# Flamingo block pair on one Trainium2 core: the openings of both attentions in another order

## What is computed

```python
x = x + tanh(g_xattn[0]) * L0_xattn(layernorm(x), ctx)       # 16 heads of 16, mask on the keys
x = x + tanh(g_ffn[0])   * L0_ffn(layernorm(x))              # 8 experts, top 2, and a shared one
x = x + tanh(g_xattn[1]) * L1_xattn(layernorm(x), ctx)       # attention, two norms, gelu layer
x = x + tanh(g_ffn[1])   * L1_ffn(layernorm(x))              # ternary weights, two norms
```

## Time and profile before

| | us |
|---|---|
| three runs | 1234.52, 1238.16, 1238.09 |
| their median | 1238.09 |
| the profiled execution, its own time | 1233.72 |
| its span, first to last instruction | 1232.0 |

### The profile page before, as it was taken

The page is one execution under the profiler, slowest core; times in us unless marked ns, Lnnn a source line. Parts: engine busy times, 40 slices in busy tenths (PEclk is TensorE's granted clock), DMA queues, the critical chain, the costliest instruction groups (busy, mean ns, idle before and its releaser), DMA issues.

```text
span 1232.0 us, 26547 instructions
## 1 busy us (share of the span) xinstructions
PE 1160.3 (94%) x9040; PEld 1085.2 (88%) x9041; DVE 990.5 (80%) x2045; ACT 781.3 (63%) x1489; POOL 676.2 (55%) x772
## 2 busy tenths in 40 slices
PE   6999999989889999999699999998999999899998
PEld 5999999879778999999689999997899998788887
DVE  6899999756897766666689999996987887888887
ACT  4777777668464555555377777775444546777874
POOL 5444333243105556553788777721454656788885
PEclk9999999979999999999899999999999999999999
DMA  4211121113102333333543333313000000000001
GB/s 129 56 53 53 53 57 57 46 61 112 52 1 61 109 106 109 104 105 97 130 74 66 68 67 62 62 30 103 5 2 0 0 0 1 9 18 26 26 26 35
DMA packets 70276, 68.74 MB, mean 56 GB/s; under 512 B 24576, under 2 KB 62208, under 8 KB 69952
## 3 DMA queue, kind: packets, MB, share of 16 engines
q1 hardware_dynamic: 55920, 47.77, 12.8%
q0 software_dynamic: 12576, 18.62, 8.1%
q10 hardware_dynamic: 1712, 1.50, 0.4%
HBM read 44.00 MB, written 18.61 MB: 51 GB/s over the span
## 4 chain that ended last, share of the span: by engine, by line
PE 74%; DVE 11%; ACT 5%; issue 5%; POOL 4%; DMA 1%; ACTq 0%; DVEq 0%; POOLq 0%; SPq 0%
PE PSUM L798 13%; PE PSUM L800 13%; PE PSUM L799 13%; PE PSUM L899 8%; PE PSUM L887 6%; PE PSUM L878 5%; PE PSUM L897 2%; POOL s_t_gh L2659 2%; PE PSUM L810 2%; PE PSUM L851 1%; PE PSUM L908 1%; PE PSUM L1959 1%; ACT s_m_xn L1456 1%; PE PSUM L2848 1%; PE PSUM L2849 1%
## 5 line engine op out<-in xcount | busy, mean ns | idle before, releaser
L2209 POOL TENSOR_TENSOR s_f_h_lo<-s_f_h,s_f_h_hi 128x512 fp32r<-128x512 f32 x64 | 93.4, 1466 | 102.9 <-ACT s_f_h_hi L2153 102.3
L1382 POOL DMA_INDIRECT s_m_tile_x<-normed_x,s_tokens x78 | 96.8, 1241 | 75.1 <-DVE s_tokens L1673 53.7
L899 PEld LDWEIGHTS PSUM<-s_a_v_diagonal,s_a_prob_t 128*128 128x128 f32 x1024 | 125.9, 192 | 0.0
L899 PE MATMUL PSUM<-s_a_v_diagonal,s_a_prob_t 128*128 128x36 f32 x1024 | 125.2, 268 | 0.0
L728 ACT ACTIVATE s_a_prob_t<-PSUM 128x640 f32<-128x640 f32 x128 | 90.0, 703 | 36.6 <-PE PSUM L887 34.9
L474 DVE TENSOR_REDUCE s_a_row_max<-PSUM 128x8 f32<-128x640 f32 x128 | 104.7, 818 | 7.3 <-PE PSUM L878 4.0
L481 DVE TENSOR_TENSOR s_a_less<-PSUM,s_a_row_max 128x640 f32<-128x640 f32 x128 | 104.9, 820 | 4.4
L1049 POOL DMA_INDIRECT s_x<-sorted_y,s_slots x60 | 95.3, 1588 | 19.7 <-issue 13.6
L2147 ACT ACTIVATE s_f_h<-PSUM,s_cols 128x512 f32<-128x512 f32 x64 | 44.0, 688 | 89.6 <-PE PSUM L800 89.0
L887 PE MATMUL PSUM<-s_ident,s_a_prob 128*128 128x128 f32 x640 | 93.7, 277 | 1.0
L798 PE MATMUL PSUM<-s_m_x_hi,s_m_up_w 128*128 128x256 f32 x312 | 91.8, 294 | 1.1 <-issue 1.0
(11 more groups left out here) (327 smaller groups left out, 4222.5 us busy)
## 6 DMA issues: line engine op xcount, KB each, us to landing
sorted_y<-s_m_tile_y SPq DMA_DIRECT2D x39, 256.0 KB
s_a_kd<-s_a_k_parts SPq DMA_DIRECT2D x126, 40.0 KB
s_x<-x SPq DMA_DIRECT2D x16, 256.0 KB, 3.1
s_a_ctx<-ctx SPq DMA_DIRECT2D x32, 128.0 KB, 2.8
s_moe_raw<-moe_w SPq DMA_DIRECT2D x16, 256.0 KB
normed_x<-s_m_xn SPq DMA_DIRECT2D x16, 256.0 KB, 3.1
y<-s_x SPq DMA_DIRECT2D x16, 256.0 KB, 2.1
s_late_raw<-moe_w SPq DMA_DIRECT2D x11, 256.0 KB, 2.9
```

Of the source, the lines that this page charges most:

```text
L899: last = pe.matmul(a.o_ps[:, 2 * c:2 * c + 2, :], a.prob_t[j % 2][:, c, :], v[:, j // BT, 0, 2 * c:2 * c + 2], start=False, stop=c == PC - ...
L1382: pool.indirect_dma_start(m.tile_x[n % 2][:, t, :], None, d["normed_x"], bass.IndirectOffsetOnAxis(ap=tokens[:, BT * n + t:BT * n + t + 1] ...
L2209: pool.tensor_tensor(f.h_lo[m % 4][:], f.h[m % 4][:], f.h_hi[m % 4][:].bitcast(F32), ALU.subtract).then_inc(f.h_split, 1)
```

## The change

Nothing is computed differently. In stage 0, ACT rounds the first block's queries before it lays the bias rows; DVE takes the query residue before the second block's norm; PE transposes the second block before it folds the bias; DVE takes the last weight residue and the bias after the second unit's maximum. In stage 1, DVE takes the second block's statistics before the first block's query residue and its norm right after it, not in the first body; ACT runs one exponential on a column of ones into an unused tile after the first queries; POOL issues the third block's first gather after `add_bias(first)` and `inverse_std(second)`, not before them. After line 302 the line numbers of the changed file differ from the old ones by up to two.

```diff
-                sb(scope, n + "gap", [P, 8])
+                self.unused = sb(scope, n + "gap", [P, 8])
...
                 value_tails(first)
+                q_residue(first)
                 ln_apply(second)
-                q_residue(first)
             else:
...
                 bias_of_output()
                 add_rows(second)
-                q_residue(first)
                 ln_stats(second)
                 ln_aggregate(second)
+                q_residue(first)
+                ln_apply(second)
 
             def body(b, behind, ahead):
...
                 score_max(b, 0)
                 less_max(b, 0)
-                if not behind:
-                    if a.stage == 0:
-                        weight_residue(2)
-                        dve.wait_ge(gates_done, 1)
-                        dve.wait_ge(a.small_in, 32)
-                        bias_of_output()
-                    else:
-                        ln_apply(second)
                 if ahead:
                     x_residue(b.next())
                 score_max(b, 1)
+                if a.stage == 0 and not behind:
+                    weight_residue(2)
+                    dve.wait_ge(gates_done, 1)
+                    dve.wait_ge(a.small_in, 32)
+                    bias_of_output()
                 if behind:
                     normalise(b.last(), 2)
                 less_max(b, 1)
...
                 mask_laid(first, j)
+            q_rounded(first)
             if a.stage == 0:
                 bias_rows()
-            q_rounded(first)
             if a.stage == 0:
                 last_weights()
+            else:
+                act.activation(a.unused[:, 0:1], ones[:, 0:1], ACT.Exp)
...
                 score(b, 1)
                 if a.stage == 0 and not behind:
-                    fold_bias()
                     pe.wait_ge(a.v_main, 1)
                     pe.wait_ge(a.v_tail, 1)
                 if ahead:
                     transpose_x(b.next())
+                if a.stage == 0 and not behind:
+                    fold_bias()
...
                 gather(second, 1, a.second_rows[1])
-                gather(third, 0)
                 pool.wait_ge(mix.y_ps, SHARED + ALL)
                 add_bias(first)
                 inverse_std(second)
+                gather(third, 0)
                 gather(third, 1)
```

## The result

| | us |
|---|---|
| kernel before, 22 runs | 1235.80 median (1233.68 to 1245.45) |
| changed kernel, 22 runs | 1240.21 median (1233.80 to 1251.67) |
| ratio | 1.0039, 95% interval 1.0025 to 1.0053 |
| profiled execution of the changed kernel, its own time | 1247.52 |
| its span | 1245.8 |

The changed kernel is slower by 4.8 us (0.0039 x 1235.8; the two medians are 4.4 apart). Its median lies in the range and 0.7 from the forecast 1239.5, but that flatters the forecast: it started from 1238.09, the median of three runs, and over 22 runs the kernel before has 1235.8. What was forecast is the difference, +1.4, and it came out at +4.8, just over the 0.3% that I called "no change".

What follows compares the result with a forecast made beforehand. PE bounds the kernel (94% of the span) except in two openings, chains of single hand-overs. Stage 0 −1.1, POOL's order +1.3 and clock +1.2 sum to +1.4: 1239.5 us from the three-run median 1238.09, range 1233.5 to 1243.0.

Steps and rivals of the forecast that it cites:

- What bounds an opening: Both stages' openings: a chain of single hand-overs between engines, where whatever is saved or lost stays so.
- Stage 0, −1.1: Opening of stage 0: the reordered chain brings the second `less_max` earlier, gain 0.6 to 1.1 us, up to 1.6.
- Stage 1, step 1, norm 2.1 earlier: Stage 1's opening: second block's early statistics and norm let its transpositions start at 611.0 instead of 613.09.
- Step 2, table 0: Stage 1, ACT: the table load of 1.28 us was already hidden, so moving it gives 0.
- The forecast 1236.8: Alternative total: a table switch costs about 2.66 us by the page; with the load open, opening 1 gains 2.7.
- Step 3, POOL's order: Stage 1: the third block's later gathers make its inverse deviation 1.3 us later than before (0.65 to 2.05).
- The landing, taken as 2.6: Stage 1: the third block's second gather waits 2.6 us for the first's rows, between bounds 1.92 and 3.34.
- a wait for DMA of one to two us: Sign on POOL in stage 1: this wait before the fourth issue in a row of L1050, about 614.9.
- The clock, +1.2: PE behind its wait before stage 1's third-block transpositions: half clock costs 1.2 us, between 0 and 3.3.
- slower than before, by one mechanism: Stage 1: third inverse deviation 2.05 us late, clock low for ten us; +4.8, giving 1242.9; chance 0.13.
- Both openings gain: Both stages: POOL doesn't stand in the way, stage 1 keeps 1.7 us; 1235.3, at best 1234.4; chance 0.25.
- The rule on the shared port: While VectorE runs a two-port operation, GpSimd can't write its DMA descriptors; trace showed hardly anything, 1.62 against 1.57.

Runs made afterwards that it cites:

- `stage0_only`: The kernel before with only the change's stage 0 steps; 1234.70 us median of 12 runs, ratio 0.9991 (0.9969 to 1.0012).
- `pool_only`: The kernel before with only POOL's new order in stage 1; 1241.43 us median of 12 runs, ratio 1.0045 (1.0030 to 1.0061).
- `bias_later`: The changed kernel with `add_bias(first)` behind `inverse_std(second)` on POOL; 1242.10 us median of 6 runs, ratio 1.0052 (1.0032 to 1.0072).
- `keep_warm`: The changed kernel with 28 idle matmuls on PE at the end of stage 1's first block; 1240.68 us median of 8 runs, ratio 1.0059.
- `f_no_table`: `pool_f` without the early exponential on ACT; 1233.91 us median of 10 runs, ratio 0.9990 (0.9977 to 1.0004).
- `pool_back`: The changed kernel with POOL's old order in stage 1's opening; 1233.97 us median of 12 runs, ratio 0.9984 (0.9965 to 1.0003).
- `late_7`: The kernel before plus seven idle powers on POOL ahead of stage 1's third inverse deviation; 1246.56 us median of 8 runs, ratio 1.0096.
- `late_7_warm`: `late_7` with 28 idle matmuls on PE while it waits for the third block's normalised rows; 1240.28 us median of 6 runs, ratio 1.0046.
- `stage1_no_pool`: The kernel before with only DVE's early second-block statistics and norm in stage 1; 1235.80 us median of 12 runs, ratio 1.0009.
- `pool_f`: The changed kernel with POOL's order third block's first gather, `inverse_std(second)`, `add_bias(first)`; 1232.93 us median of 12 runs, ratio 0.9986.
- the three late kernels: `late_7`, `late_7_warm` and `late_4`, the kernel before with four idle powers ahead of stage 1's third inverse deviation (1241.90 us, ratio 1.0045).
- `f_warm`: `pool_f` with idle matmuls on PE in three places of stage 1's opening; 1234.02 us median of 12 runs, ratio 1.0000 (0.9983 to 1.0017).

## Why the prediction came out as it did

- **What bounds an opening: right.** A chain of hand-overs, where a loss stays. The keys of the third block start 4.3 us later than before in the profile (636.68 for 632.36), and the next ones of stage 1 7.9 (654.63 for 646.77); they stay 7.8 behind to the last (811.87 for 804.04).
- **Stage 0, −1.1: order right, size not shown.** The fold left the chain and the transpositions follow the scores. The second `less_max` started at 23.39, not 22.1, because PE gave the last query product at 14.92, not 14.20, and the scores took 1.97. Counted from that product it came 0.5 earlier than before (8.47 for 8.98). The forecast took the clock of one execution for the kernel's. `stage0_only` can't tell −1.1 from 0; the means over all the profiled executions, 35.7 for 36.8, fit −1.1 without showing it.
- **Stage 1, step 1, norm 2.1 earlier: too much.** It was 0.9. The step took `add_rows` at its old 0.69 in its new company; started just behind `add_bias` it takes 1.83 (`pool_only` 1.67; 0.69 in `bias_later`, and in `keep_warm`, where it started first). POOL started the second inverse deviation at 609.42 for the forecast 607.6.
- **Step 2, table 0: right.** The load ran at 608.67, in the gap foreseen, and `f_no_table` shows no difference. The forecast 1236.8 by the Trainium skill's figure ("ScalarE: Activation LUTs", What ACT_TABLE_LOAD costs) falls with it: the load takes 1.28 and the exponential starts 1.29 behind its start, here too.
- **Step 3, POOL's order: the right cause.** `pool_only` has the loss, `pool_back` doesn't. The landing, taken as 2.6, was 2.48 and 2.59 (the sign "a wait for DMA of one to two us" didn't follow from that 2.6). But since POOL came to it 1.8 later, the second gather started at 616.72 for 614.85, and the third inverse deviation 2.4 later than before by its start (629.47 for 627.03) and 3.0 by DVE's norm that waits for it (631.09, where the kernel before had 628.05), for the forecast 1.3. This is the first mis-sized term.
- **The clock, +1.2: the second mis-sized term.** I took a slow stretch over keys and values, in one place. Profiled it lasts from 631 into 651 and adds 4.8 between the third block's transpositions and the next keys (2.9 in `pool_only`), on top of 2.8 of lateness (3.8). `late_7` against `late_7_warm` shows directly that clock of this size can hang on such a wait: 5.4 against 0.1. How the 4.8 of the medians split is not shown. Among the 22 runs of the changed kernel a line through time and granted clock falls 0.95 us per 0.001; at 0.979, the median clock of the kernel before, it gives 1237.2, where the same line through 85 runs of the kernel before gives 1235.2: 2.0 for waits and 2.8 for clock. But the 12 runs of `pool_only` give 1239.6 by the same reading, 4.4 for waits, and the median clock tells the kernels apart only in part: 0.975 for the changed kernel and `pool_only`, 0.979 for `pool_back` and `pool_f`, but also 0.976 and 0.977 for `stage1_no_pool` and `stage0_only`, which lost nothing.
- **The rivals.** What happened is the second one, "slower than before, by one mechanism", to which I gave 0.13: third inverse deviation over two us late, slow clock for ten us, and +4.8. I held the long slow stretch for unlikely because that of stage 0 had been short; the nearer row was the one of stage 1 itself, 0.51 over ten us after a wait half as long. "Both openings gain" needed the gather out of the way; `pool_f` does that, and even so its gain over the kernel before, 1.7 us by the ratio, is inside the interval.
- **The rule on the shared port.** The sentence of the Trainium skill ("SBUF — State Buffer", SBUF: two separate sides) was taken for descriptors and weighed as nearly nothing. Single issues were a little longer (1.76 to 2.07 for 1.54 to 1.57); that DVE's work made them so is not shown, since the one of 612.67 in the changed kernel had such work beside it too and took 1.57. What cost more was something else: two additions of 128x512, one on DVE and one on POOL, that met, 1.83 for 0.69.

What stays open: the size of the stage 0 gain; why idle matmuls bring 6.2 us back in `late_7` and nothing in the median of the changed kernel; when the clock falls behind an opening, since it did so in some kernels without a long wait; the offset of the three late kernels.

## What to carry to other kernels

An issue that another transfer waits for belongs where its engine is idle anyway, ahead of a wait, not behind it: moving one indirect gather behind a 1.7 us wait cost 2.5 us of landing time in full and some 5 us at the end. Before moving an operation earlier, ask what will run beside it; its length in the new company is not that of the old row, and 0.03 us decide which of two meeting additions waits. And where the engine that bounds the kernel waits for more than a few us, add the slow clock behind the wait from the nearest row in the same place, at its full length. A gain in an opening can be lost again in the same way: count it only from where the engine runs at full clock.

## What the runs showed of the hardware

- Two f32 additions of 128x512, one on VectorE (0.69 us alone) and one on GpSimd (1.25 with no addition beside it, 606.59 in `bias_later`), don't share the time when they meet: the later one waits. VectorE's took 1.83 and 1.67 when it started 0.01 and 0.17 behind, and each time ended 0.56 behind the end of GpSimd's, which took 1.28 (the changed kernel, `pool_only`). GpSimd's took 1.78 when it started 0.03 behind VectorE's, which took 0.69 (`keep_warm`).
- From the end of a gather's last issue to the issue that waited for its landing 2.47 to 2.59 us passed where the first gather was issued late, behind the inverse deviation or the addition (the changed kernel, `pool_only`, `bias_later`, `keep_warm`), and 3.10 to 3.55 where it was issued early, right behind other gathers (`pool_f`, `pool_back`). The early place hides the longer landing; the late one shows the shorter.
- A wait of 4.3 to 5.8 us of TensorE ahead of the third block's transpositions in `late_7`, `pool_only`, `bias_later` and the changed kernel was followed each time by a granted clock of 0.50 in 631 to 641. With idle matmuls in the wait it was 1.00 (`keep_warm`, `late_7_warm`), but in `f_warm` the low clock came later instead.
- Executions of one kernel spread with their granted clock: 1233.8 us at 0.981 and 1251.67 at 0.969 for the changed kernel.
